# Nine merges on GpSimd, the experts' second biases by matmul and their low parts on VectorE, in a transformer layer with experts on one core

## The reference

```python
h = layernorm(x)
a = attention(layernorm(h, ln1_w, ln1_b))      # 16 heads of 128, rotary, causal; + bo
h1 = h + a
t = layernorm(h1, ln2_w, ln2_b)
raw = softmax(t @ w_gate)                      # 4 experts
top_vals, top_idx = top_k(raw, 2)
w = softmax(top_vals)
comb = zeros.at[top_idx].add(w)                # gate of each token and expert
hmid = gelu(einsum('td,edi->tei', t, we1) + be1)
eout = einsum('tei,eid->ted', hmid, we2) + be2
m = einsum('te,ted->td', comb, eout)
out = x + tanh(g_ffn) * (h1 + m)
```

## Time and profile before

| what | us |
|---|---|
| median of 3 runs (463.11 to 465.21) | 463.28 |
| the profiled execution | 467.53 |
| its span, first to last instruction | 465.7 |
| PE busy in the span | 415.1 (89%) |
| DVE busy | 364.4 (78%) |
| POOL busy | 301.2 (65%) |
| ACT busy | 286.3 (61%) |

### The profile page before, as it was taken

One profiled execution on the slowest core, in us unless ns is written; L12 is line 12 of the kernel. 1 busy time (PEld: TensorE's weight loads), 2 busy tenths in 40 slices (PEclk: granted clock), 3 DMA queues, 4 the chain that ended last, 5 costly groups with the idle time before them and its releaser, 6 DMA issues.

```text
span 465.7 us, 10305 instructions
## 1 busy us (share of the span) xinstructions
PE 415.1 (89%) x3135; PEld 361.4 (78%) x3150; DVE 364.4 (78%) x1124; ACT 286.3 (61%) x655; POOL 301.2 (65%) x433
## 2 busy tenths in 40 slices
PE   0477997998899899999999999999999996598994
PEld 0366876886776799899899898998998986586994
DVE  3854568677789797897798788888888877928997
ACT  3357674755235777587677677677677675375440
POOL 5898959720598487587587687677677555343551
PEclk9999999999999899999999999999999998989998
DMA  5600000200256875775865865855955655000011
GB/s 153 189 3 2 1 3 2 92 2 1 46 113 125 174 149 119 174 150 108 203 143 106 189 136 118 196 131 108 225 119 109 145 80 112 4 0 2 1 45 45
DMA packets 71795, 44.53 MB, mean 96 GB/s; under 512 B 57424, under 2 KB 60112, under 8 KB 71760
## 3 DMA queue, kind: packets, MB, share of 16 engines
q1 hardware_dynamic: 67680, 35.42, 36.1%
q10 hardware_dynamic: 4080, 8.69, 6.5%
HBM read 13.68 MB, written 1.05 MB: 32 GB/s over the span
## 4 chain that ended last, share of the span: by engine, by line
PE 68%; DVE 17%; issue 5%; ACT 4%; POOL 3%; DMA 2%; ACTq 0%; SPq 0%; DVEq 0%; POOLq 0%
PE bank L1464 36%; PE bank L1532 5%; PE bank L1582 5%; DVE yacc L1309 3%; PE bank L1531 3%; PE bank L1583 3%; DVE yacc L1318 2%; PE bank L1404 2%; PE bank L1445 2%; POOL room L523 2%; PE bank L1359 2%; PE bank L1380 2%; PE bank L1405 1%; DMA qk_room<-qk_room 1%; PE bank L1426 1%
## 5 line engine op out<-in xcount | busy, mean ns | idle before, releaser
L799 ACT ACTIVATE probs<-sm,nm 128x128 f32<-128x128 f32 (+1 forms) x128 | 57.0, 447 | 44.1 <-DVE nm L1184 43.8
L789 ACT ACTIVATE probs<-turned 128x768 uint16<-128x768 uint16 x60 | 64.7, 1078 | 18.1 <-DMA turned<-halves 16.5
L1464 PE MATMUL bank<-hH,qk_parts 128*128 128x512 f32 x240 | 75.4, 395 | 0.0
L536 POOL COPY halves<-probs 128x768 uint16<-128x768 uint16 x64 | 52.6, 822 | 33.0 <-DVE probs L1208 31.1
L523 POOL TENSOR_TENSOR room<-room,qk_room 128x512 f32<-128x512 f32 x32 | 41.2, 1290 | 35.6 <-DMA qk_room<-qk_room 30.6
L1464 PE MATMUL bank<-hL,qk_parts 128*128 128x512 f32 x120 | 57.7, 481 | 0.9 <-DVE room L1105 0.9
L1464 PEld LDWEIGHTS bank<-hH,qk_parts 128*128 128x128 f32 x240 | 45.2, 188 | 9.5
L1105 DVE SCALAR_TENSOR_TENSOR room<-bank,qk_bias,cst_sb 128x512 f32<-128x512 f32 x64 | 47.5, 742 | 0.0
L1076 DVE TENSOR_REDUCE nxm<-bank 128x2 bf16<-128x512 f32 (+1 forms) x48 | 32.8, 688 | 18.1 <-PE bank L1405 17.5
L523 POOL TENSOR_TENSOR room<-room,q_room 128x512 f32<-128x512 f32 x32 | 41.1, 1287 | 5.5 <-DMA q_room<-q_room 5.5
L684 ACT ACTIVATE probs<-bank 128x512 f32<-128x512 f32 x48 | 28.3, 595 | 25.4 <-PE bank L1421 14.4
(11 more groups left out here) (241 smaller groups left out, 1291.8 us busy)
## 6 DMA issues: line engine op xcount, KB each, us to landing
qk_room<-qk_room SPq DMA_DIRECT2D x64, 128.0 KB, 2.4
q_room<-q_room SPq DMA_DIRECT2D x64, 128.0 KB, 2.4
stg<-in_wqkv ACTq DMA_DIRECT2D x6, 768.0 KB, 5.8
stge<-in_we ACTq DMA_DIRECT2D x7, 256.0 KB, 3.1
stg<-in_wqkv SPq DMA_DIRECT2D x2, 768.0 KB, 5.2
stgo<-in_wo ACTq DMA_DIRECT2D x6, 256.0 KB, 3.4
x_sb<-in_x SPq DMA_DIRECT2D x4, 256.0 KB, 4.1
turned<-halves SPq DMA_TRANSPOSE x64, 2.8
```

The lines of the kernel that those rows point to most:

```text
L536: pool.tensor_copy(halves[:, j % 2, :, :], PR[:, j % 2, 0:384].bitcast(U16).rearrange("p (n h) -> p h n", h=2)).then_inc(s["b_split"], 1)
L789: act.activation(*merged(j - 3), ACT.Copy).then_inc(s["b_merge"], 1)
L799: ins = act.activation(PR[:, q, a:e], sm[:, q, a:e], ACT.Exp, bias=nm[:, q, t:t + 1], scale=-1.0, accum_out=rs[:, q, t:t + 1])
L1464: ins = pe.matmul(outp, l, r, start=(m == 0), stop=(m == n - 1))
```

## The change

- `PTs` gets four slots in place of two, and `LATE` becomes NU - 9: the merges of units 55 to 63 are POOL's. In POOL's step T the merge of unit T-3 stands behind split(T). The merge waits for the values' product of four units earlier, no longer of two.
- DVE takes maxima one unit ahead from T = 58 on: maxima(T+1) stands ahead of normalise(T). After the last step o_low(58) stands ahead of normalise(63), and the last o_low stand earlier among the phases of `second_norm`.
- `hidden_low2` and `middle_low` are DVE's. DVE's order is: output_add(30), output_add(31), phase 0 of the norm of batches 2 and 3, hidden_low2(0), hidden_low2(1), the other phases, then the low parts 0 and 1, hidden_low2(2) and (3), the low parts 2 and 3, and only then the copy of the logits.
- The be2 sums leave DVE: 12 small DMAs early in SP's queue load be2 rows, POOL makes a high and a low part of them in steps 16 to 20 (five instructions of 256 columns), PE turns the packed gates and multiplies them with these rows (4 matmuls of 256 columns for each half of the tokens), and DVE adds the product from PSUM once for each batch.
- `yacc * tanh(g) + x` is made ahead of the experts' sums (`residual_form`), the gates are scaled by tanh(g)/2, and the second softmax becomes a Tanh: ACT does it at n = 5, behind GELU 4, instead of an exponential at n = 4 ahead of it.

The diff, cut to its core (declarations, names and waits that follow from it are left out):

```diff
-        PTs = probs[:, 2:4, :]
+        PTs = probs[:, 2:6, :]
...
-            return (PTs[:, u % 2, 0:384].bitcast(U16).rearrange("p (n h) -> p h n", h=2),
+            return (PTs[:, u % 4, 0:384].bitcast(U16).rearrange("p (n h) -> p h n", h=2),
...
-        LATE = NU - 4
+        LATE = NU - 9
... sync
+            sp.wait_ge(s["q_parts"], 2 * B)
+            for q in range(4):
+                for r in range(3):
+                    row = 32 * q + E * r
+                    sp.dma_start(be2_raw[row:row + E, :], be2).then_inc(s["d_be"], 16)
             sp.wait_ge(s["wv_ready"], 1)
... gpsimd
-                pool.wait_ge(s["b_pv"], u - 1)
+                pool.wait_ge(s["b_pv"], u - 3)
                 pool.tensor_copy(*merged(u)).then_inc(s["late_merge"], 1)
+            def bias_rows(n):
...
+                if i == 2 and j < 5:
+                    bias_rows(j)
+                if U * i + j - 3 >= LATE:
+                    merge(U * i + j - 3)
...
             split(NP - 1, 6)
+            merge(NU - 5)
+            split(NP - 1, 7)
             merge(NU - 4)
-            split(NP - 1, 7)
...
-            hidden_low2(0)
-            hidden_low2(1)
-            for n in range(2 * NE):
-                if n in (2, 3):
-                    hidden_low2(n)
-                middle_low(n)
... scalar
-                if unit(i, j, 3):
+                if unit(i, j, 3) and not (isinstance(i, int) and U * i + j - 3 >= LATE):
                     merge(i, j)
...
+                if n == 5:
                     act.wait_ge(s["c_gdiff"], 1)
-                    act.activation(gate[:, 400:408], gate[:, 392:400], ACT.Exp).then_inc(s["c_gexp"], 1)
+                    act.activation(gate[:, 400:408], gate[:, 392:400], ACT.Tanh, scale=-0.5).then_inc(s["c_gexp"], 1)
... vector
-                if unit(i, j, 0) and not (isinstance(i, int) and T == 0):
+                if unit(i, j, 0) and not (isinstance(i, int) and (T == 0 or T > AHEAD)):
                     maxima(i, j)
+                if isinstance(i, int) and T >= AHEAD:
+                    maxima(*divmod(T + 1, U))
...
             normalise(NP - 1, 6)
+            o_low(NP - 1, 6)
+            normalise(NP - 1, 7)
             output_add(LAST, 0)
-            normalise(NP - 1, 7)
-            o_low(NP - 1, 6)
...
             output_add(LAST + 3, 3)
-            for phase in range(6):
+            second_norm(2, 0, 2)
+            hidden_low2(0)
+            hidden_low2(1)
+            for phase in range(1, 6):
                 second_norm(2, phase, 2)
+            middle_low(0)
+            middle_low(1)
+            hidden_low2(2)
+            hidden_low2(3)
+            middle_low(2)
+            middle_low(3)
             dve.wait_ge(s["c_logit"], 1)
             dve.tensor_copy(nh[:, 0, :], bank[5][:, 0:256]).then_inc(s["c_lgT"], 1)
+            residual_form(0)
+            residual_form(1)
...
-            for m in range(2 * E):
-                        ins = dve.scalar_tensor_tensor(yacc[:, n, :], be2_rows[:, e, :], gate[:, 4 * n + e:4 * n + e + 1], yacc[:, n, :],
-                                                       ALU.mult, ALU.add)
...
+            middle_low(5)
+            accumulate(0)
+            middle_low(6)
+            accumulate(1)
+            middle_low(7)
+            dve.tensor_copy(gates_turned, bank[4][:, 0:256]).then_inc(s["c_gT"], 1)
+            residual_form(2)
+            residual_form(3)
+            add_biases(0)
+            accumulate(2)
+            for m in range(3, 2 * E):
+                middle_low(2 * m + 2) if m < 2 * E - 1 else None
+                middle_low(2 * m + 3) if m < 2 * E - 1 else None
+                accumulate(m)
+                if m == 5:
+                    add_biases(1)
... tensor
-            expert_out(0)
+            expert_out(0, (0,))
             pe.wait_ge(s["c_lgT"], 1)
...
+            expert_out(0, (1,))
             expert_out(1)
             middle(4)
             middle(5)
             middle(6)
+            middle(7)
+            pack_turn()
+            expert_out(2)
...
+                if n == 8:
+                    second_bias(0)
+                if n == 12:
+                    second_bias(1)
```

More of the change, by code:

```diff
@@ L857, in _ @@
             steps(act, step, 2, NU - 2)
-            merge(NP - 1, 6)
             exponentials(NP - 1, 6)
+            o_high(NP - 1, 6)
             exponentials(NP - 1, 7)
-            o_high(NP - 1, 6)
             o_high(NP - 1, 7)
@@ L1296, in _, with accumulate @@
             link(dve.tensor_tensor(Gt(0, 32), Gt(120, 32), Gt(152, 32), ALU.add))
-            dve.wait_ge(s["d_be"], 16)
-            dve.wait_ge(s["b_yadd"], NU // 2)
-            for m in range(2 * E):
+            packed = nh[:, 1, :].rearrange("p (t b w) -> p b t w", t=2, w=32)
+            gates = gate[:, 0:32].rearrange("p (b t e) -> p b t e", b=B, e=E)
+            link(dve.tensor_copy(packed[:, :, :, 0:E].bitcast(F32R), gates))
+            dve.tensor_copy(packed[:, :, :, 2 * E:3 * E], packed[:, :, :, 0:E])
+            dve.tensor_tensor(packed[:, :, :, E:2 * E].bitcast(F32R), gates, packed[:, :, :, 0:E], ALU.subtract).then_inc(s["c_pack"], 1)
+            def accumulate(m):
                 c, e = divmod(m, E)
@@ L1581, in step @@
                         pe.wait_ge(s["b_oL"], T - 5)
[L1582 to L1583 removed]
+                    pe.matmul(value_bank(j)[:, 0:256], V[:, 2 * b, r * HD:(r + 1) * HD], PTs[:, j % 4, 0:256], start=True, stop=False)
+                    pe.matmul(value_bank(j)[:, P:256], V[:, 2 * b + 1, r * HD:(r + 1) * HD], PTs[:, j % 4, 256:384], start=False, stop=True).then_inc(s["b_pv"], 1)
                 if v_event(i, j):
@@ L1630, in middle, with expert_out @@
                 middle_part(n, 0, 512).then_inc(s["c_mid"], 1)
-            def expert_out(m):
+            def expert_out(m, parts=(0, 1)):
                 c, e = divmod(m, E)
@@ L1636, in expert_out @@
                     pe.wait_ge(s["b_yadd"], NU // 2)
-                for hf in range(2):
+                for hf in parts:
                     if m >= 2:
@@ L1644, in expert_out, with pack_turn, second_bias @@
                     ins.then_inc(s["c_exp_pe"], 1)
+            def pack_turn():
+                pe.wait_ge(s["c_pack"], 1)
+                for t in range(2):
+                    ins = pe.transpose(bank[4][:, t * P:(t + 1) * P], nh[:, 1, t * P:(t + 1) * P], ident)
+                ins.then_inc(s["c_pack_pe"], 1)
+            def second_bias(c):
+                if c == 0:
+                    pe.wait_ge(s["c_gT"], 1)
+                    pe.wait_ge(s["be2_step"], 5)
+                else:
+                    pe.wait_ge(s["c_badd"], 2)
+                for hf in range(2):
+                    rows_ = slice(32 * (2 * c + hf), 32 * (2 * c + hf) + 3 * E)
+                    for t in range(2):
+                        ins = pe.matmul(bank[4 + hf][:, 256 * t:256 * (t + 1)], gates_turned[rows_, t * P:(t + 1) * P], be2_parts[rows_, :],
+                                        start=True, stop=True)
+                ins.then_inc(s["c_be"], 1)
             pe.wait_ge(s["we_ready"], NP // 2)
@@ L1674, in _ @@
             middle(6)
-            for n in range(7, 2 * NE):
+            middle(7)
+            pack_turn()
+            expert_out(2)
+            for n in range(8, 2 * NE):
                 middle(n)
+                if n == 8:
+                    second_bias(0)
+                if n == 12:
+                    second_bias(1)
                 if n % 2:
```

101 lines of the change are left out of this document (64 added, 37 removed).

## The result

The changed kernel took 467.1 us (median of 7 runs) where the kernel before, run beside it, took 464.16: a ratio of 1.0065 with a 95% interval of 1.0041 to 1.0089. One of the seven, 473.37 us, was a slow run, which the ratio leaves out. Measured a second time, with 12 runs, the ratio was 1.0043 (1.0005 to 1.0081). So it is slower by about 2 to 3 us. The prediction was 463.8 us, +0.1%; its range, to 467.2, holds the measured time by 0.1 us, which is luck as much as foresight.

What follows compares the result with a forecast made beforehand. PE was taken to bound the loop and pace the experts, queue order the drain, DVE the end. 467.53 + 2.4 drain + 0.8 experts' queue - 2.9 end + 0.2 loop = 468.0, +0.1%: 463.8 us on the median 463.28, range 460.0 to 467.2.

Steps and rivals of the forecast that it cites:

- Drain: From 372 us to the first expert product: late merges on POOL move that product from 405.89 to 408.3, +2.4 us.
- I take both again, since PE waits as long in both layouts: Drain and first expert products: the old run's two half-clock parts stay; full clock in both would give 2.8 us.
- second rival: Drain: PE's clock falls in new gaps, two stretches add +2 to +3 us, 465.8 to 466.8; chance 0.2.
- The prediction's own sign: PE's clock in the new trace: the prediction is wrong if it differs in more than the two half-clock stretches.
- The base: Starting time of the sum: the profiled run's 467.53 us, with the result then put on the median of 463.28.
- The loop: Loop over units: POOL's five bias instructions in steps 16 to 20 reach PE by 0 to 1 us, taken as 0.2.
- The experts' queue: PE's queue in the experts: 2.0 us of new waits and work less 1.2 saved, +0.8 us, between 0 and 1.0.
- The end: After PE's last matmul: DVE's lag falls from 3.83 to 0.9 us, a gain of 2.9.
- rival that DVE becomes the bound: Experts: DVE's strict order makes it the bound, the end keeps half its lag, +1.5, 465.3 us; chance 0.06.
- Tanh: Experts, on ACT after GELU 4: Tanh taken to share GELU's table load, cost 0.
- third rival: Experts, on ACT: Tanh takes its own table load, +1.9, 465.7 us; chance 0.07.
- Breaks even: Drain: leading maxima and four slots let merges come early enough, 461.4 us, or 458.6 at full clock; chance 0.22.

Runs made afterwards that it cites:

- c2: The changed kernel once more, no edit, for a second profile: 468.2 us, ratio 1.0043 to the kernel before.
- e8: Changed kernel with unused extra PE matmuls in the waits ahead of units 55, 58, 60 and the first expert product: 465.36 us, ratio 0.9998.
- c1: The kernel before once more, no edit, for a second profile: profiled execution 463.95 us, median of ten runs 466.73.
- e2: Changed kernel with the drain of before, experts' part and four `PTs` slots kept: 465.01 us, ratio 0.9982 to the kernel before.
- e5: Kernel before with only the leading maxima and the new order of the drain's last steps on DVE and ACT: 463.15 us, ratio 0.9953.
- e6: Changed kernel with merges 55 to 59 on ACT, `hidden_low2` on POOL, bias rows behind the drain, logits' copy ahead of low part 2: 460.11 us, ratio 0.9887.
- e7: Changed kernel with merges of units 58 to 63 on POOL and 55 to 57 on ACT: 465.92 us, ratio 0.9986 to the kernel before.
- e3: Changed kernel with unused extra PE matmuls in its waits for POOL's merge ahead of units 55, 58 and 60: 466.65 us, ratio 1.0026.

## Where the prediction was right and where it was wrong

**Drain: the chain right, the clock wrong.** The first expert product was predicted for 408.3 and stands at 408.30, but that is chance. This execution reached the scores of unit 60 1.29 us earlier; from there the forecast was 33.0 us (408.3 - 375.26), and 34.33 and 33.81 were measured. Step by step the queue of POOL did what was laid out: merge 55 behind the rotary subtraction and split 58, PE waiting 3.20 us for it (2.7 forecast), 1.88 ahead of unit 58 (2.5), 0.99 ahead of unit 60 (1.9; 1.91 in c2, which has no stretch just ahead of it), the turn at 404.06 (403.95). With PE's clock kept full (e8) the drain is 32.12 us against 29.54 in c1: +2.6, where the forecast had +2.4.

The step that failed is "I take both again, since PE waits as long in both layouts". The old profile's two stretches were taken as a constant of both kernels. They are not: before's drain has none in c1, and the changed drain got one or two behind the new waits, which cost 1.7 to 2.3 us (33.81 and 34.33 against 32.06). That is the second rival, with the place and the price that it named; it had a chance of 0.2. Its time, 465.8 to 466.8, is what the first ratio gives on 463.28: 466.3 (the second gives 465.3). The prediction's own sign, that the clock differs in more than the two stretches, has come too.

**The base.** The sum was made on an execution 4.3 us above the median of three runs and then scaled. Against c1 its span has 3.6 us more: 1.76 up to the scores of unit 60 (375.26 and 373.50), with the stretch near 156 us; 1.09 in the drain; and 0.76 in the experts, where half clock covered all of the first products. Such surplus belongs to the execution and not to the kernel. The stretch near 156 us is in six of the thirteen profiles, of kernels with the change and without (before, c2, e2, e5, e6, e7); from the scores of unit 6 to those of unit 12 PE takes 28.8 to 29.4 us in these and 27.2 to 27.7 in the others. The first profile of the changed kernel lacks it, c2 has it. The prediction saw the gap between 467.53 and 463.28 and did not ask which rows made it.

**The loop: 0.2 taken, 0.8 measured.** The bias rows were known to cost up to 1; the value was taken near the lower bound, with the loop called PE-bound. The wait is that of one unit, where PE needs a low part of the weights that POOL, with ACT between, now makes too late.

**The experts' queue: 0.8 taken, about 1.0 measured.** The wait at `expert_out(2)` is 0.71 us (0.8 forecast), the one half way through `expert_out(0)` 1.52 (1.8). The wait of 1.39 ahead of `expert_out(1)` before is gone, as forecast.

**The end: 2.9 taken, 2.91 measured**, DVE 0.92 us behind PE (0.9). A low part takes DVE 0.69 us (0.7). PE has no wait of note behind 431.29, as forecast. The rival that DVE becomes the bound falls.

**Tanh.** No table load stands between GELU 4 and GELU 5; ACT from the load made for GELU on:

```profile
422.28 1.28 ACT L908 ACT_TABLE_LOAD   x1
...
426.91 0.63 ACT L913 ACTIVATE o_parts<-G 128x512 fp32r<-128x512 f32 x1
427.45 0.19 ACT L903 ACTIVATE gate<-gate 128x8 f32<-128x8 f32 x1
427.59 0.69 ACT L908 ACTIVATE G<-bank,cols_sb 128x512 f32<-128x512 f32 x1
```

The third rival falls. The Trainium skill, ScalarE: Activation LUTs, section "Table sets: the hidden batching unit", lists tanh with the sets of exp and of sigmoid and does not name it for that of gelu. The trace decides here: Tanh ran at 427.45 under the load of 422.28.

**Breaks even**, the first rival, falls: the drain is 2.6 us longer at full clock. The four slots don't help as long as merge 55 can't start before split 58 ends.

The sum as it stands: +0.8 loop, +2.6 drain, +1.0 PE's expert queue, -2.9 end, that is +1.5 at equal clock, where the forecast had +0.5; most of that gap is the loop. One run of c2 and five of before at nearly full clock agree (464.33 against 462.24 to 463.42). Measured were 2.9 us (467.1 - 464.16) and 2.5 (468.2 - 465.72). The difference, 1.0 to 1.4, is of the size by which half clock in the new drain (1.7 to 2.3) exceeds what it costs the old one in some of its executions (1.1, 30.63 against 29.54). An estimate from the mean clock of each run fits: c2's runs have 8.9 us at half clock on average, those of before beside them 9.3, of which some 3 lie behind PE's last matmul (2.5 in the first profile, 3.5 in c1); so the changed kernel has about 2.5 us more of it in PE's work, worth up to 1.3 at half the speed. Where these stretches stand in runs without a profile isn't known, so this last part of the sum is argued, not shown.

## What to carry to other kernels

Before a sum is made on a profiled execution, compare its time with the median of more than three runs, and name the rows that make up the difference; a half-clock stretch in one execution is no constant, neither of this kernel nor of the next. In a drain, where each engine works through a short chain, busy shares (ACT 61%, POOL 65% before) don't say what moving an operation between engines costs: the question is what stands ahead of it in that queue at that moment. And an order that pulls work ahead (the leading maxima, worth 2 us here when taken alone) should be measured apart from the move that it was bundled with.

## What was not expected of the hardware

Where PE's waits in the drain were filled with matmuls, its clock stayed at 2.4 GHz there in the profiles of e3 and e8, and fell to 1.2 behind the next long wait that was left (e3, 3.17 us ahead of 406.77); with that one filled as well, it didn't fall (e8). In c1 a wait of 2.54 us in the drain was followed by full clock, in the first profile of before a wait of 2.56 us at the same place by half clock; what decides between them these runs don't show. And Tanh needed no table load of its own behind GELU.
